# Softmax before the transposes, value rows as the stationary operand, and a new order on all engines

## The reference, cut to what matters

```python
for i in range(6):
    x = attn_layer(shift_tokens(x), Wqkv[i], q_scale[i], k_scale[i], Wo[i]) + x
    x = ffn_layer(shift_tokens(x), ln_g[i], ln_b[i], W1[i], b1[i], W2[i], b2[i]) + x

# attn_layer: 16 heads of 64, windows of 32 tokens that see their own and the previous window
q, k = rotate(l2norm(q) * qs), rotate(l2norm(k) * ks)
sim  = einsum('bhwie,bhwje->bhwij', q, k) * 8        # 32 queries x 64 keys in each window
attn = softmax(where(mask, -big, sim), -1)
out  = einsum('bhwij,bhwje->bhwie', attn, v)
return out.reshape(b, n, 1024) @ Wo
# ffn_layer: LayerNorm, x @ W1 (128 -> 2*341), a * gelu(gate), @ W2 (341 -> 128)
```

## Time and profile before

| | us |
|---|---|
| time, median of 3 runs | 4081.42 |
| lowest and highest | 4073.69, 4090.21 |
| the profiled execution, its time | 4086.48 |
| its span, first to last instruction | 4084.7 |
| TensorE busy in the span | 3511.6 (86%) |
| VectorE | 2906.8 (71%) |
| ScalarE | 2390.6 (59%) |
| GpSimd | 2086.5 (51%) |
| mean granted TensorE clock | 0.948 of full speed |

### The profile page before, as it was taken

How to read it: one execution, slowest core, us unless ns; L and a number is a source line. 1 busy time by engine, 2 the same in 40 slices (tenths; PEclk the granted TensorE clock), 3 DMA queues, 4 the chain that set the end, 5 groups by cost and what they waited for, 6 DMA issues and landing times. The chain is left out here.

```text
span 4084.7 us, 157400 instructions
## 1 busy us (share of the span) xinstructions
PE 3511.6 (86%) x63228; PEld 2234.6 (55%) x63228; DVE 2906.8 (71%) x5185; ACT 2390.6 (59%) x4206; POOL 2086.5 (51%) x2011
## 2 busy tenths in 40 slices
PE   4889898898898888986996689998898898888897
PEld 2556565565565655662221466665565665555564
DVE  3778787787787777873232678887787787787783
ACT  2566665665666656652663456666565565565563
POOL 3556565566565555551001556555556565556551
PEclk7999999999999999997998899999999999999998
DMA  3223223223233222320001322332323322322221
GB/s 95 72 59 97 66 71 88 71 72 85 64 75 91 65 71 69 76 59 3 1 1 32 79 69 70 86 75 77 84 67 80 75 70 78 83 68 69 67 67 37
DMA packets 194569, 273.85 MB, mean 67 GB/s; under 512 B 59788, under 2 KB 85640, under 8 KB 192264
## 3 DMA queue, kind: packets, MB, share of 16 engines
q1 hardware_dynamic: 193800, 263.23, 25.4%
HBM read 35.57 MB, written 1.05 MB: 9 GB/s over the span
## 5 line engine op out<-in xcount | busy, mean ns | idle before, releaser
L1083 POOL TENSOR_TENSOR qkn<-rot,rn 128x512 f32<-128x512 f32 x768 | 784.8, 1043 | 971.6 <-DVE rn L944 971.6
L1077 POOL TENSOR_TENSOR rot<-t 128x512 f32<-128x512 f32 x768 | 977.7, 1273 | 389.2 <-DVE t L923 351.6
L922 DVE TENSOR_TENSOR t<-ps,table 128x512 f32<-128x512 f32 x768 | 528.0, 687 | 297.6 <-ACT sq L733 214.4
L733 ACT ACTIVATE sq<-ps 128x512 f32<-128x512 f32 x768 | 457.4, 596 | 288.0 <-PE ps L508 286.0
L766 ACT ACTIVATE oT<-ps 128x512 f32<-128x512 f32 x384 | 213.6, 596 | 621.6 <-PE ps L582 621.0
L506 PE MATMUL ps<-w_hi,in_hi 128*128 128x512 f16 x1152 | 454.2, 394 | 120.0 <-POOL w_lo L1103 75.6
L923 DVE TENSOR_TENSOR t<-ps,table 128x512 f32<-128x512 f32 x768 | 523.0, 681 | 0.0
L927 DVE TENSOR_REDUCE n<-sq 128x8 f32<-128x512 f32 x768 | 487.5, 677 | 0.0
L970 DVE TENSOR_TENSOR on<-ps,rsum 128x512 f32<-128x512 f32 x384 | 247.5, 687 | 333.7 <-PE ps L572 331.9
L572 PE MATMUL ps<-arena,pT 64*32 64x64 f32 x24576 | 317.7, 228 | 168.5 <-issue 167.7
L507 PE MATMUL ps<-w_lo,in_hi 128*128 128x512 f16 x1152 | 450.9, 391 | 0.0
(11 more groups left out here) (125 smaller groups left out, 5507.1 us busy)
## 6 DMA issues: line engine op xcount, KB each, us to landing
arena<-arena SPq DMA_DIRECT2D x1152, 128.0 KB, 2.4
arena<-arena SPq DMA_DIRECT2D x768, 64.0 KB, 2.0
w_stage<-in_L_ffn_Wqkv SPq DMA_DIRECT2D x12, 1536.0 KB, 6.9
wo_sb<-in_L_ffn_Wo SPq DMA_DIRECT2D x12, 512.0 KB, 5.9
xsh<-xs SPq DMA_DIRECT2D x48, 128.0 KB, 2.7
f_in<-xs SPq DMA_DIRECT2D x48, 128.0 KB, 2.4
xsh<-xs SPq DMA_DIRECT2D x48, 127.8 KB, 2.4
f_in<-xs SPq DMA_DIRECT2D x48, 127.8 KB, 3.1
```

The lines of the kernel that those rows point to most:

```text
L733: act.activation(sq[:, c, :], proj[c % 2][:, :], ACT.Square).then_inc(act_sq, 1)
L922: dve.tensor_tensor(t1[:, b, :].rearrange("p (h d) -> p h d", d=DH), src, cos, ALU.mult)
L1077: pool.tensor_tensor(rot[:, c, :], t1[:, c % 2, :], t2[:, c % 2, :], ALU.add).then_inc(pool_add, 1)
L1083: pool.tensor_tensor(qkn[:, 0, c, :].rearrange("p (h d) -> p h d", d=DH), rot[:, c, :].rearrange("p (h d) -> p h d", d=DH), rn[:, c, :].un ...
```

## The change

Five things are changed.

1. **Probabilities are normalised before they are transposed.** `out_norm` on the outputs is gone. `prob_norm` multiplies the probabilities by the inverse sum, one half (8 heads) on DVE and one half on POOL.
2. **The operands of `outputs` are swapped.** A block of `vw`, 64 keys by 64 columns, is the weights, and 32 columns of pT stream. The result comes out with channels on the partitions, so `turn_out` (8 transposes a tile) and the buffer `on` are gone; ACT copies `sv` to oT directly.
3. **The two `sv` banks are one tensor of 1024 columns**, so `shift_max` is one reduction and one subtraction; `norm2` becomes two reductions of 1024 columns instead of four of 512.
4. **The centring** of the LayerNorm is one matmul with `centre_w` (identity minus 1/128) and a copy by ACT, in place of a matmul with `mean_w` and a subtraction on DVE.
5. **The order in `step` is new on every engine.** `scores` and `shift_max` move from tile T-2 to T-1, at the end of the step; inverse norm and three of the four `normalise` move into the tile's own step. ACT runs the three GELUs of a batch in one step with one pair of table loads instead of two.

```diff
 def outputs(T, B, s):
-    pe.wait_ge(dve_sub, tile_done(T, 1, 2))
+    pe.wait_ge(dve_sub, tile_done(T))
     pe.wait_ge(act_p, tile_done(T, 1, 2))
     wait_apart(pe, v_loaded[s], windows_done(B))
-    for pair in range(PAIRS):
+    for j in range(4):
         for w in range(WPT):
-            for par in range(2):
-                r = slice(par * KEYS, (par + 1) * KEYS)
-                last = pe.matmul(sv[par][w * WIN:(w + 1) * WIN, pair * DH:(pair + 1) * DH],
-                                 pT[r, pair, w * WIN:(w + 1) * WIN], vw[r, v, w, pair * DH:(pair + 1) * DH],
+            for half_of, par in ((0, 0), (1, 1), (0, 1), (1, 0)):
+                r = slice(half_of * KEYS, (half_of + 1) * KEYS)
+                last = pe.matmul(sv[half_of][par * DH:(par + 1) * DH, j * P + w * WIN:j * P + (w + 1) * WIN],
+                                 vw[r, v, w, j * P + par * DH:j * P + (par + 1) * DH],
+                                 pT[r, 4 * par + j, w * WIN:(w + 1) * WIN],
                                  start=True, stop=True, skip_group_check=True)
     last.then_inc(pe_pv, 1)
-def turn_out(T):
...
 def turn_prob(T, p, followed):
+    for par in range(2):
+        if followed:
+            pe.wait_ge(act_k, tile_done(T + 1, par, 4))
+        pe.wait_ge(*((dve_pn, tile_done(T)), (pool_pn, tile_done(T)))[par])
...
 def scores(T, s):
-    pe.wait_ge(dve_on, tile_done(T - 1, 1, 2))
+    pe.wait_ge(act_o, tile_done(T - 1, 1, 2))
...
 def shift_max(T, p):
+    src = sv_all[:, :].rearrange("q (n k) -> q n k", k=KEYS)
+    dve.tensor_reduce(smax[:, :], src, axis=AX.X, op=ALU.max).then_inc(dve_max, 1)
+    dve.wait_ge(dve_max, tile_done(T))
+    dve.tensor_tensor(prob[:, p, :, :, :].rearrange("q a n k -> q (a n) k"), src,
+                      smax[:, :].unsqueeze(2).broadcast_to([P, HEADS, KEYS]), ALU.subtract).then_inc(dve_sub, 1)
...
-def out_norm(T, p):
+def prob_norm(T, p):                                   # DVE; its twin on POOL takes rsum[:, p, HPC:HEADS]
+    dve.wait_ge(dve_rs, tile_done(T))
+    dve.tensor_tensor(prob[:, p, 0, :, :], prob[:, p, 0, :, :], bc(rsum[:, p, 0:HPC], KEYS),
+                      ALU.mult).then_inc(dve_pn, 1)
...
 def store_out(T, B, s):                                # ACT
     act.wait_ge(pe_wo, batch_done(B - 1, s // 2, 2))
+    act.wait_ge(pe_pv, tile_done(T))
+    for half_of in range(2):
+        act.activation(oT[:, half_of::2, s * P:(s + 1) * P],
+                       sv[half_of][:, :].rearrange("p (j t) -> p j t", j=4), ACT.Copy).then_inc(act_o, 1)
...
+def f_centre(B):                                       # now on ACT
+    act.wait_ge(pe_mean, batch_done(B))
+    act.wait_ge(act_xg, batch_done(B - 1))
+    act.activation(xc[:, :], fa[:, :], ACT.Copy).then_inc(act_xc, 1)
```

343 lines of the change are left out of this document (160 added, 183 removed).

## The result

The changed kernel takes 3798.98 us (median of 4 runs, 3792.34 to 3812.88), the kernel before in the same session 4082.21 us (4073.69 to 4090.21). The ratio is 0.9328, 95% interval 0.9302 to 0.9353: 6.7% faster. The prediction said 3760 us; the time lies 39 us above it and inside 3560 to 3980.

A forecast was written before the change was run, and what follows sets the result against it. TensorE was taken as nearest the bound, 15.3 us of work in an 18.4 us step, the rest waits. Terms of -0.87 + 0.3 - 0.8 - 0.35 = -1.72 us, times 190, gave 3760 us from 4086.5; range 3560 to 3980.

The forecast's parts named there:

- turn_out, -0.87 us a step: On TensorE, the 8 output transposes of each tile go, saving 0.87 us a step, all of it counted.
- outputs, +0.3: On TensorE, swapped operands mean 64-column weight loads, making the 1.50 us `outputs` stage 0.3 us a step longer.
- Rival A: In `outputs`, 64-column loads go two at a time: 3.8 us instead of 1.8, 4060 us in all; chance 0.07.
- Issue stops, -0.35: TensorE's stops for instructions in the bursts of `outputs` and `scores` fall from 1.2 to 0.85 us a step.
- Rival B: TensorE's instructions run out in every step, each burst costing 2.1 us: 4396 us in all; chance 0.05.
- Dependency waits, -0.8: Waits from the chain through one tile fall from 1.3 us a step to 0.4 in the GELU step and 0.1 elsewhere.
- The GELU step, 0.4 left over: On ACT, GELUs and table loads delay one step in four by 1.5 us, booked as 0.4 us a step.
- Boundary, 0: At layer boundaries, where TensorE waits for w_lo, the change makes no difference, within 3 us at ten boundaries.
- DVE 13.5 and POOL 11.8 us a step: Busy time per step: DVE falls from 14.6 to 13.5 us, POOL rises from 10.7 to 11.8.
- "Worth nothing by itself": DVE's saving of 1.1 us a step lies below TensorE, so it was counted as nothing in the sum.
- Rival C: The chain of one tile, a loop of 14.0 to 15.1 us, bounds the kernel: 3930 to 4120 us; chance 0.18.
- Rival D: Everything fits: stops 0.3 us a step and no dependency waits, 3497 us in all; chance 0.08.

The follow-up runs named there:

- e10: The changed kernel with the `outputs` burst cut in two, k's transposes and a gate piece between, and k's copy ahead of the output's on ACT: 3740.3 us.
- e5: The changed kernel with the GELU replaced by a plain copy with the same bias, so without table loads: 3789.2 us.
- e9: The changed kernel with DVE's row maximum of tile T-1 taken ahead of the small work of `inv_norm`, the subtraction staying behind it: 3864.0 us.
- e6: The changed kernel with both halves of the probabilities normalised on DVE, none on POOL: 3950.1 us.
- e11: e10 with `scores` cut in two as well, the second part behind the value projection: 3817.2 us.
- e4: All new operations of the changed kernel, but in the order of the kernel before on every engine: 5848.7 us, ratio 1.435 to the kernel before.
- e1: The changed kernel with the operands of `outputs` turned back, 32 columns of pT loaded and 64 value columns streaming: 3776.4 us.

## Why the prediction was right, and where not

- **turn_out, -0.87 us a step**: right in kind; alone, in the old order, it measured -0.69.
- **outputs, +0.3**: right in kind and a little small. The stage from first to last start is 1.85 us, predicted 1.6 to 2.0, but without a stop it was 1.25 to 1.32 before, not 1.50; its busy time rose by 0.5 us a step. Alone the swap measured +0.39 in the old order and +0.12 in the new. Rival A (over 3 us) is out.
- **Issue stops, -0.35**: the two bursts are 227 us before and 129 after, -0.5 a step; with stops at other lines 248 and 186.5, -0.32. That looks like the forecast but isn't: 56 us of the 248 were the waits for pT's copy, which are dependency. Real stops went from 192 to 184.5 us, -0.04 a step: 44 us less inside the two bursts, nearly as much more at other lines. This is the term that was mis-sized; the working took every "issue" row for a stop, and counted on stops that overlap with another wait. Rival B (over 500 us) is out: `scores` start 2.7 us behind the last start of `outputs` in the median tile (7.7 before), and yet most bursts meet no stop. How long a burst is and what stands ahead of it does matter, as e10 shows.
- **Dependency waits, -0.8**: nearly right, by a working that was not. All waits of TensorE other than issue are 313.7 us before and 237.0 after; with those for pT's copy 370 and 239, -0.69 a step. The forecast's 1.3 "dependency" was a remainder: 18.4 less 15.3 of work, 1.2 of stops and 0.6 of boundary. TensorE's own waits for ACT and DVE in the kernel before (58.0 + 29.1 + 28.4 us in the rows above, and 56 ahead of `outputs`) are 0.9 us a step; the rest of the 1.3 was work. The windows say so too: TensorE is busy (1578.1 + 1602.1)/192 = 16.6 us a step, not 15.3. That was the work of one light step, and the next step of the same kernel has 0.9 us more (start and end, length, busy us of TensorE):

```profile
1119.27:1136.37 17.10, 15.49 (x328) 1.00 0.26 64
1136.37:1153.50 17.13, 16.38 (x381) 1.00 0.39 95
```

  Of the 0.9, 0.7 went, where the forecast took 0.8 off its 1.3.
- **The GELU step, 0.4 left over**: too large. TensorE waits 36.8 us for it in all, 0.2 us a step, and without table loads the kernel is not measurably faster (e5).
- **Boundary, 0**: TensorE's wait for w_lo went from 75.6 to 87.1 us, 0.06 a step.
- **DVE 13.5 and POOL 11.8 us a step**: measured 14.2 and 12.3. The operations were counted rightly, but the exclusion between the two engines was left out: 0.5 us a step for POOL's half, and some 0.7 for DVE (378 - 186, 214 - 192, 289 - 238 and 632 - 193 ns in the four small instructions of the norms).
- **"Worth nothing by itself" for DVE, POOL's half and the order**: right for this change, by luck of place. Much of the exclusion's cost fell where DVE would have waited anyway (e9). As a rule it is wrong: one half more on DVE, held up by POOL, costs 0.79 us a step (e6).
- **Rival C**, the chain: TensorE's waits at the probabilities are 13.1 us for DVE (and 3.9 for POOL), under the 100 named. But the loop of 14.0 us was rightly called tight: the subtraction 0.35 us later on average (e9) goes with 0.34 us more a step, and `scores` ending later with 0.4 (e11 over e10). **Rival D** is out: the stops stayed.

The sum against the measurement, in us of the profiled execution: predicted -327, measured -274 in span. Work -108 predicted (0.57 x 190) and -129 measured; waits -218 predicted and -138 measured. The 53 us that are missing are 80 us of waits that did not go, less 21 us of work saved beyond the forecast and some 6 us of gaps too short to be listed. Of the 80, 59 belong to the stops (0.35 x 190 = 67 predicted, 7 measured) and 21 to the dependency waits (152 and 131). That the time came within 39 us of the forecast is in part luck: work and a remainder that was too large made up for the stops.

The steps without GELU and stop were to be near 15.0 us: the shortest of each s are 14.0, 15.7, 15.5 and 16.1 us, 15.3 on average. TensorE's busy share rose from 86% to 89%, as the forecast wanted.

## What to carry to other kernels

Take the waits that a change can remove from the waiting engine's own rows, not from the difference between a long step and a short one. Look at an "issue" wait ahead of a group's first instruction twice: the code says what it waits for, and the timeline whether that had just ended. An operation moved ahead of a transpose or another consumer needs a new order first (here 26 to 44% hang on it), and in such an order the place of an instruction counts more than its length: work that stands where its engine would wait anyway can be had for nothing, even when another engine holds it up, and the same work behind that wait lengthens the chain. An edit that makes TensorE wait can also cost clock, and then its own work slows too (`outputs` by 213 us in e4). Bursts of hundreds of tiny matmuls are worth cutting up between large ones, as long as nobody waits for the end of the burst: that was another 59 us.

## What the runs showed of the hardware

- The DVE instruction on `rn`, with two SBUF operands and 192 ns long alone, ended 45 to 52 ns after POOL's `add` whenever it began inside it, 87 times in 87. POOL's instruction on the probabilities, 1.04 us alone, took 1.55 on average where it began 0.05 us behind such a DVE instruction of 0.69, 189 times in 192. DVE instructions with one operand in PSUM kept their 686 ns beside POOL.
- 128 records of `outputs` with blocks of 64 x 64 float32 in four parts of the array follow each other in about 14.5 ns (1.85 us). With blocks of 64 x 32 it is 12.4 ns (1.58 us) in e1, where each part comes twice within four matmuls, and about 10 ns (1.25 to 1.32 us) in the order of the kernel before.
- Stops for want of instructions stay at fixed places of a program, up to 2.1 us long in the changed kernel; 128 more instructions at the start of the program moved them to other steps and left the time. All 108 inside the two bursts of the changed kernel end 1.15 to 1.65 us behind the end of a packet of 16384 bytes in the `instruction` queue. A shorter burst also shortens the stop in the next one (0.86 to 0.24 us in the step shown). How many instructions TensorE holds in store stays open.
- Where TensorE stood for 4.42 and 2.38 us in a step of e4, the granted clock behind it was 0.50, and `outputs` took 3.64 us.
